# Local attention in a fused kernel: scores of a window as one 128 by 128 product with the heads' queries on the diagonal, instead of four 32 by 32 products

## What is computed

```python
xw = x.reshape(b, w, p, c)                     # p = 32 tokens, c = 128
qkv = xw @ w_qkv.T + b_qkv
sim = jnp.einsum('bwphd,bwqhd->bhwpq', q, k) * scale   # scale = 32 ** -0.5
sim = sim + rel_pos[:, idx][None, :, None]
sim = jnp.where(mask[None, None], -jnp.inf, sim)
probs = jax.nn.softmax(sim, axis=-1)
out = jnp.einsum('bhwpq,bwqhd->bwphd', probs, v)
out = out.reshape(b, w, p, N_HEADS * HEAD_DIM) @ w_out.T + b_out
```

## Time and profile before

| | us |
|---|---|
| median of 3 runs | 1574.26 (1573.67 to 1580.92) |
| the profiled execution | 1575.33 |
| its span, first to last instruction | 1573.5 |
| busy PE, DVE, POOL, ACT | 1217.1, 964.4, 572.9, 545.5 |
| w1, without its expert products | about 841 to 982 |
| w2, with the routing of four images | about 983 to 1121 |

### The profile page before, as it was taken

One profiled execution on the slowest core, in us unless ns is written; L12 is line 12 of the kernel. 1 busy time (PEld: TensorE's weight loads), 2 busy tenths in 40 slices (PEclk: granted clock), 3 DMA queues, 4 the chain that ended last, 5 costly groups with the idle time before them and its releaser, 6 DMA issues. The chain is left out here.

```text
span 1573.5 us, 31944 instructions
## 1 busy us (share of the span) xinstructions
PE 1217.1 (77%) x11770; PEld 1058.2 (67%) x11770; DVE 964.4 (61%) x2351; ACT 545.5 (35%) x1247; POOL 572.9 (36%) x643
## 2 busy tenths in 40 slices
PE   6999988468581999879896584757549999999940
PEld 3555547468580999879894354535539999998940
DVE  3777763798654444435543775686556777887731
ACT  3444431064350555434453341432313233222220
POOL 4000000100235666655502552045516640556654
PEclk9999997779555999989997796679559999999975
DMA  7700000000401333233324220011103332333341
GB/s 270 281 0 1 1 1 3 4 1 0 128 21 59 100 119 115 85 105 106 105 70 104 51 67 17 1 32 41 42 27 97 112 103 72 110 103 103 88 140 53
DMA packets 87887, 115.45 MB, mean 73 GB/s; under 512 B 18693, under 2 KB 70272, under 8 KB 87744
## 3 DMA queue, kind: packets, MB, share of 16 engines
q1 hardware_dynamic: 66784, 62.73, 13.0%
q0 software_dynamic: 20960, 50.76, 10.2%
HBM read 53.01 MB, written 60.42 MB: 72 GB/s over the span
## 5 line engine op out<-in xcount | busy, mean ns | idle before, releaser
L1302 POOL DMA_INDIRECT sorted_rows<-s_normed,s_places x128 | 138.1, 1079 | 164.5 <-DMA sorted_rows<-s_normed,s_places 51.8
L1378 POOL DMA_INDIRECT sx_fetch<-sorted_results,s_places x128 | 135.6, 1059 | 142.3 <-DMA sx_fetch<-sorted_results,s_places 62.8
L1302 POOL DMA_INDIRECT sorted_rows<-g_normed,g_places x128 | 134.3, 1049 | 106.9 <-DMA sorted_rows<-g_normed,g_places 48.8
L1461 PE MATMUL g_bank<-weights,gx_hT 128*128 x1360 | 168.7, 278 | 0.6 <-issue 0.6
L1461 PEld LDWEIGHTS g_bank<-weights,gx_hT 128*128 128x128 f32 x1360 | 161.5, 195 | 1.2 <-issue 1.2
L1378 POOL DMA_INDIRECT gx_fetch<-sorted_results,g_places x128 | 124.7, 974 | 102.4 <-DMA gx_fetch<-sorted_results,g_places 71.0
L1426 PE MATMUL s_bank<-sx_xT_high,sx_w_now 128*128 128x256 f32 (+1 forms) x510 | 151.6, 297 | 1.8 <-DVE sx_hT L1531 1.2
L1428 PE MATMUL s_bank<-sx_xT_high,sx_w_now 128*128 128x256 f32 (+1 forms) x510 | 143.9, 282 | 0.0
L1427 PE MATMUL s_bank<-sx_xT_low,sx_w_now 128*128 128x256 f32 (+1 forms) x510 | 143.8, 282 | 0.0
L1486 ACT ACTIVATE gx_hT<-g_bank,gx_b_now 128x256 f32<-128x256 f32 x340 | 133.1, 482 | 3.0 <-PE g_bank L1461 3.0
L1461 PE MATMUL s_bank<-weights,sx_hT 128*128 (+1 forms) x1020 | 130.5, 278 | 3.5 <-issue 1.7
(11 more groups left out here) (409 smaller groups left out, 2792.0 us busy)
## 6 DMA issues: line engine op xcount, KB each, us to landing
sorted_rows<-zeros POOLq DMA_DIRECT2D x29, 512.0 KB, 16.6
gx_xq<-sorted_rows SPq DMA_DIRECT2D x85, 128.0 KB, 2.1
sorted_results<-gx_yq SPq DMA_DIRECT2D x85, 128.0 KB, 1.9
sx_xq<-sorted_rows SPq DMA_DIRECT2D x85, 128.0 KB, 2.1
sorted_results<-sx_yq SPq DMA_DIRECT2D x85, 128.0 KB, 2.0
feats<-in_x SPq DMA_DIRECT2D x8, 512.0 KB, 6.2
out<-s_normed SPq DMA_DIRECT2D x16, 256.0 KB, 3.8
g_raw_up<-in_L_ffn_W SPq DMA_DIRECT2D x1, 2048.0 KB, 9.1
```

The source lines that it names most:

```text
L1302: pool.indirect_dma_start(out=sorted_rows[g], out_offset=bass.IndirectOffsetOnAxis(ap=places[:, at, r:r + 1], axis=0), in_=normed[:, at, : ...
L1378: pool.indirect_dma_start(out=fetch[n % 2][:, i, r, :], out_offset=None, in_=self.sorted_results[g], in_offset=bass.IndirectOffsetOnAxis(a ...
L1461: done = pe.matmul(down[u % 2][:, P * k:P * k + C], hT[u % 2][0:width, i, P * k:P * k + P], self.w_down[0:width, bass.ds(e, 1), i, :].rear ...
```

## The change

The scores of a window are one product: the stationary operand is a 128x128 block with the four heads' queries on its diagonal and zeros elsewhere, the moving operand the window's 128x32 keys. So 16 products per half take the place of 64. `qT` becomes one buffer of 16 such blocks (128 x 2048 float32) in place of two of 128 x 512. DVE clears it once in each stage, after `normalise(0)`. ACT fills the diagonal with four activations of 32 partitions x 512 in place of one of 128 x 512, and, as there is one buffer, first waits for the scores of the half just before. The mixing is as it was.

```diff
-        self.qT = [take(f"qT{i}", HALF) for i in range(2)]
+        self.qT = take("qT", HEADS3 * HALF).rearrange("p (w i q) -> p w i q", w=CW, i=HEADS3)
@@
+        self.q_cleared = t.sem(f"{tag}q_cleared")
@@ def scores(b, h):
-            by_window(score, qT[h], kT[h]).then_inc(self.score_ready, 1)
+            for w in range(CW):
+                at = slice(WINDOW * w, WINDOW * w + WINDOW)
+                done = pe.matmul(score[:, at], qT[:, w, :, :].rearrange("p i q -> p (i q)"), kT[h][:, at],
+                                 start=True, stop=True)
+            done.then_inc(self.score_ready, 1)
@@ def take_qk(b, h):
-            if b >= 1:
-                act.wait_ge(self.score_ready, b * 2 + h - 1)
-            act.activation(qT[h][:, :], proj[0][:, :], ACT.Identity, bias=qbias[:, 0:1], scale=HD ** -0.5
-                           ).then_inc(self.q_taken, 1)
+            if b >= 1 or h == 1:
+                act.wait_ge(self.score_ready, b * 2 + h)
+            else:
+                act.wait_ge(self.q_cleared, 1)
+            for i in range(HEADS3):
+                part = slice(HD * i, HD * i + HD)
+                done = act.activation(qT[part, :, i, :], proj[0][part, :].rearrange("p (w q) -> p w q", w=CW),
+                                      ACT.Identity, bias=qbias[part, 0:1], scale=HD ** -0.5)
+            done.then_inc(self.q_taken, 1)
@@ def vector(self, dve, ...):
         normalise(0)
+        dve.memset(self.qT[:, :, :, :].rearrange("p w i q -> p (w i q)"), 0.0).then_inc(self.q_cleared, 1)
```

## The result

| | before | after |
|---|---|---|
| median, us | 1575.41 (1573.67 to 1580.92, 4 runs) | 1610.95 (1609.13 to 1614.23, 4 runs) |
| the profiled execution | 1575.33 | 1611.02 |
| its span | 1573.5 | 1609.3 |
| up to the first transpose of w1 (first L1850/L1851) | 847.4 | 846.0 |
| w1, from there to the first transpose of w2 | 142.6 | 157.2 |

The change makes the kernel 1.0222 times as long, interval 1.0191 to 1.0253: 35.5 us. All of it lies in the two stages, 14.6 in w1 and 22.7 in w2. The forecast had the sign and the place, and 20.4 us for the size. The measured time is inside its range of 1583 to 1620, but not inside the 1586 to 1602 of its main case A: it lies where the forecast has rival B, in which the clock falls.

The account below looks back on a forecast made before the run. It took no engine as full: the two stages are chains passing between engines. w1's 6.7, w2's 11.8 and the clearing's 1.9 sum to 20.4 us, giving 1594.5 us; the 8-in-10 range was 1583 to 1620.

Parts of the forecast that it names:

- main case A: Whole kernel: the forecast itself holds, 1586 to 1602 us; chance 0.63.
- rival B: Middles of w1 and w2: the clock falls, ten score runs at half clock, 34 us more, 1603 to 1640; chance 0.17.
- the clearing: DVE's memset of the diagonal buffer: hidden in w1, all on the path in w2, 1.9 us.
- runs at full clock since this window is granted 0.92: Middle of w2: steps priced at full clock, each score run 3.5 us.
- by nothing to spare: w1: scores(3, 0) ends 9.5 us late, just hidden by DVE's wait for gathered rows; only the tail's 6.7 us shows.
- ACT's copies: Both stages: four query copies 0.57 us apart take 2.4 us after the scores; PE waits 1.1 us in h = 1 steps.
- The price of a run: Score runs: the weight load sets a record's cost, so 32 records take 3.5 us at full clock, 7.0 at half.
- rival C: Score runs: moving columns set the cost, so runs stay short and the kernel is not slower, 1571 to 1581; chance 0.08.
- The stops: PE's waits without semaphore inside runs, taken for instruction supply: they go with fewer records, worth 3.0 us on the path.
- rival D: PE's stream: its stops stay and nothing is given back, 3 us more, 1598 and up to 1604; chance 0.12.
- Both tails: Last score run of each stage at half clock, 7.0 us: +6.7 us in w1, +3.95 in w2.
- a w1 that ends over 10 us later: Listed sign that the forecast is wrong; it expected w1 to end some 6.7 us later.

Follow-up runs that it names:

- double_wide: The changed kernel with two diagonal query buffers, so ACT copies early, and 128 moving columns per score product instead of 32; 1588.83 us, ratio 1.0091 to the kernel before.
- double: The changed kernel with two diagonal query buffers, both cleared, so ACT's query copies start early again; 1600.85 us, ratio 1.0193 to the kernel before.
- wide: The changed kernel with 128 moving columns per score product instead of 32, the extra ones overwritten later; 1596.59 us, ratio 1.0147 to the kernel before.
- tail: The changed kernel with only each stage's last score run, scores(3, 1), again as 64 products of 32x32x32; 1600.02 us, ratio 1.0152 to the kernel before.
- act_only: The changed kernel's diagonal buffer, clearing and four late ACT copies, but scores again as 64 products of 32x32x32; 1582.01 us, ratio 1.0052 to the kernel before.
- double_wide_late_tail: double_wide_late with each stage's last score run again as 32x32 products; 1588.71 us, ratio 1.0099 to the kernel before.
- double_wide_late: double_wide with the clearing moved behind DVE's share of the router's normalisation; 1585.13 us, ratio 1.0089 to the kernel before.
- pe_only: The kernel before with only its scores as 16 products of 128x128 by 32 columns on plain queries, attention scores not computed; 1590.45 us, ratio 1.0098.

## Why the prediction was right and where it was wrong

The time was in the range, but the sum was not right: 20.4 us against 35.5. The range held because it took in the lower half of rival B, and the excess is not only B's: 7.9 us of it are in w1, where wide runs take only 2.2 back. That the time fell where B has it is so in part luck.

Step by step in w2, growth over before:

| step | predicted, us | measured, us |
|---|---|---|
| the clearing | 1.9 | 2.1 |
| further, up to scores(1, 0) | 0 | 0.6 |
| scores(1, 0) to project(2, 0) | 3.4 | 4.1 |
| project(2, 0) to project(2, 1) | 0.4 | 3.3 |
| project(2, 1) to project(3, 0) | 1.4 | 2.0 |
| project(3, 0) to project(3, 1) | 0.65 | 4.2 |
| project(3, 1) to give(2, 0) | 2.0 | 2.3 |
| give(2, 0) to the end of the stage | 3.95 | 4.2 |

- **The step that failed** is "runs at full clock since this window is granted 0.92". The clock of the kernel before was carried over to one whose runs move 32 columns in the time of 128. The runs did stay at full clock. The projects behind them did not, and the two rows that are off by most, 2.9 and 3.6 us, are those in which project(2, 0) and project(3, 0) grew by 2.6 each. Rival B named the cause and priced it in the wrong place: ten runs at half clock, 34 us. double_wide against double, and wide against after, with the runs' length at full clock and the copies left as they were, settle that the columns matter: 12 to 16 and 12 to 14 us. What part of the 2.6 us of each project is the run and what part the wait for ACT ahead of it was not separated; tail shows that it can also be missing.
- **w1** was the second step that failed: 6.7 predicted, 14.6 measured. I had the slack before the last adds used up "by nothing to spare", so each further microsecond went straight to the end. Of PE in w1, after:

```profile
940.49 0.41 PE L2345 MATMUL g_bank<-ident,s_raw 128*128 128x128 f32 x2 [3.20 <-DVE weights L2373]
...
941.17 4.44 PE L1860 MATMUL g_bank<-g_normed,w_wT 128*128 128x512 f32 x6
...
959.92 3.65 PE L1879 MATMUL g_bank<-g_normed 128*128 128x32 f32 x32
...
974.16 6.87 PE L1879 MATMUL g_bank<-w_kT,g_normed 128*128 128x32 f32 x32
```

  scores(3, 0) starts 14.3 us later than in the earlier trace rows, or 15.7 counted from the start of the stage, where I had 7.8. The projects (1, 1) to (3, 1) ahead of it grew by 5.9 us together; the one in the second row is project(3, 0), 2.73 us before. And ahead of the turned weights PE waits 3.20 us for DVE's split, which stands behind ACT's copies, a queue that I had charged with 0.8. Over the steps from turn_batch(2) to scores(3, 0) such waits come to 14.4 us, before to 8.2. double and wide weigh these: early copies take 9.1 us of w1's growth back and the waits to 8.9; wide runs take back 2.2, all of it in the last run, and leave the waits at 14.4. act_only, late copies behind short runs, has waits of 13.6 and has grown by 3.2. So in w1 it is the late copies behind long runs, in w2 as much the clock (9.1 us back with wide, 5.9 with double, each from one profile). How much of w1's queue is its order and how much the clock under it was not separated.
- **ACT's copies**: predicted 2.4 us and 0.57 apart, measured 2.75 and 0.69. The pitch was taken from two copies of 128 partitions. The queries are ready 2.85 us after the run instead of 2.45, and PE waits 1.25 and 1.51 us instead of 1.1, which is 0.15 and 0.4 us in two of the rows above.
- **The price of a run** was right: 3.5 and 7.0 predicted from the earlier trace rows, 3.65 and 6.87 measured, the same with 32 and with 128 columns. That refutes rival C: the moving columns do not set the distance, and what 8, 32 and 128 columns share is the load.
- **The stops** went, as predicted, and rival D is refuted. They come back where short runs stand next to each other (act_only, tail, double_wide_late_tail), in mixes whose code is unchanged, so they go with the number of instructions and not with a wait. That it is the supply of instructions that runs short remains my reading: no view shows what PE waits for in them. The Trainium skill ("Runtime: NRT & Kernel Launch", "Instruction fetch mechanics") has the fetch hidden behind dispatch; if these stops are the fetch, the traces disagree, with 1.54, 1.88 and 1.82 us of it.
- **The clearing** was 0.2 off: 1.76 us, and 0.37 ahead of it, and the path grew by 2.1. The Trainium skill's rule ("VectorE: DVE Perf Modes", "Zero memsets can be issued as uint32 (trn2)") gave an estimate of 2.1 us, and the traces agree: two of them in a row start 2.14 us apart (double_wide_late, 1003.99 and 1006.13). Two slips of the working change nothing: in straight proportion the bounds from the earlier trace rows are 1.32 and 2.45 us, not 1.24 and 2.35, and the terms ahead of give(2, 0) add up to 8.0, not 8.1.
- **Both tails** ran at half clock, as assumed; w2's row is 0.25 off.
- **The signs**: what I had listed as a sign of being wrong, "a w1 that ends over 10 us later", did appear; no loss came after the stages.

## What to carry to other kernels

Four small products that sat side by side on the array were not a waste to be cleaned up: packing them on a diagonal pays a full weight load for each window, 0.11 us a record at full clock, and turned runs of 1.3 to 2.2 us into 3.65. Where a full load is paid anyway, it is worth trying to let the product move more columns, even useless ones that are overwritten: here 128 instead of 32 cost nothing and gave back 9 to 16 us, and the rows have it come through the clock. And price the clock for what stands behind the changed work, not for that work alone, and a slack once for all changes that draw on it.

## What the runs showed that was not expected

- 128 moving columns take no longer than 32 (both 3.65 us for 32 records), and with them the granted clock over w2's middle steps is 0.93 to 1.00 instead of 0.81 to 0.91. Of project(2, 0), (3, 0) and (3, 1), after has two at 5.46 us, tail one at 5.35, double one at 4.54 and pe_only one at 4.41, the last two with no wait ahead; all versions with wide runs have all three at 2.81 to 2.84. act_only, with short runs, has two at 4.51 and 4.54.
- The clock rises within a wide run that begins low: the last run took 5.12 us in w2 (double_wide_late; clock 0.50 up to 1115.7, 1.00 from 1116.7 on) and 4.27 in w1 (wide), where after has 6.87 in both.
- Four ACT copies of 32 partitions by 512 start 0.69 us apart, as long as each takes, while two of 128 partitions start 0.57 apart. They also write every fourth block of 32 columns. Which of the two makes them keep their distance was not tried.
